# A tuned attention-and-FFN block: the order in which the output projection's weight operands are made, and where one constant load and one bank wait stand

## The reference

```
xn   = layernorm(x)
q, k, v = split(xn @ w_qkv)                  # 32 query heads, 8 key/value heads, D = 128
s    = (q @ k.T) / sqrt(128) - slope[head] * sqrt(i - j), masked where j > i
attn = softmax(s) @ v
out  = x + attn @ w_o                        # attn: 2048 x 4096, w_o: 4096 x 1024
         + xn @ W.T + b + lora(xn, top-1 rank by a gate)
```

## Time and profile before

| | us |
|---|---|
| median of 3 runs (2544.09 to 2546.38) | 2545.13 |
| the profiled execution's own time | 2546.86 |
| its span, first to last instruction | 2545.1 |
| projections, up to the last step's end | about 1208 |
| attention with the output projection, from there on | about 1337 |
| PE busy / DVE / ACT / POOL | 2422.9 / 1514.5 / 1386.5 / 782.1 |
| mean granted TensorE clock | 0.980 of 2.4 GHz |

### The profile page before, as it was taken

The page is one execution under the profiler, slowest core; times in us unless marked ns, Lnnn a source line. Parts: engine busy times, 40 slices in busy tenths (PEclk is TensorE's granted clock), DMA queues, the critical chain, the costliest instruction groups (busy, mean ns, idle before and its releaser), DMA issues.

```text
span 2545.1 us, 35024 instructions
## 1 busy us (share of the span) xinstructions
PE 2422.9 (95%) x12128; PEld 2057.6 (81%) x12128; DVE 1514.5 (60%) x2817; ACT 1386.5 (54%) x3075; POOL 782.1 (31%) x1030
## 2 busy tenths in 40 slices
PE   5999999997899999999699999999999999999999
PEld 4787888886778888888588788887887878878787
DVE  5657455565656446554566666666666666666665
ACT  4432143334533133333767777677776777777764
POOL 3211000001221000000434545345444454454634
PEclk9999999998999999999899999999999999999999
DMA  4546354555245435454655555554655555655543
GB/s 147 186 133 221 118 181 153 186 207 199 93 143 206 166 134 198 166 198 153 223 186 203 187 194 185 202 194 169 220 187 198 187 175 207 207 182 200 182 166 125
DMA packets 118257, 455.95 MB, mean 179 GB/s; under 512 B 11946, under 2 KB 12090, under 8 KB 109121
## 3 DMA queue, kind: packets, MB, share of 16 engines
q1 hardware_dynamic: 86032, 334.11, 38.0%
q0 software_dynamic: 32048, 119.60, 13.5%
HBM read 276.96 MB, written 176.69 MB: 178 GB/s over the span
## 4 chain that ended last, share of the span: by engine, by line
PE 84%; DVE 5%; ACT 4%; POOL 3%; issue 2%; DMA 2%; ACTq 0%; DVEq 0%; SPq 0%; POOLq 0%
PE ps L636 27%; PE ps L637 26%; PE ps L638 26%; PE ps L823 5%; POOL wo_raw L618 1%; POOL op_lo L594 1%; DMA lora_lo<-lora_s 1%; ACT probs L1023 1%; ACT res_hi L883 1%; ACT pt_hi L883 1%; DVE stats L1132 1%; ACT rows L912 1%; DVE pt_lo L1118 1%; DVE w_lo L1118 1%; DVE res_b L1118 0%
## 5 line engine op out<-in xcount | busy, mean ns | idle before, releaser
L883 ACT ACTIVATE w_hi<-raw 128x1024 fp32r<-128x1024 f32 x196 | 207.3, 1061 | 559.6 <-PE ps L638 440.6
L1118 DVE TENSOR_TENSOR w_lo<-raw,w_hi 128x1024 fp32r<-128x1024 f32 x196 | 239.2, 1224 | 358.6 <-ACT w_hi L883 358.5
L1386 DVE TENSOR_TENSOR acc<-ps,acc 128x512 f32<-128x512 f32 x448 | 298.8, 688 | 256.5 <-issue 229.2
L636 PE MATMUL ps<-x_hi,w_hi 128*128 128x512 f32 x1120 | 436.5, 390 | 0.0
L637 PE MATMUL ps<-x_lo,w_hi 128*128 128x512 f32 x1120 | 435.9, 389 | 0.0
L638 PE MATMUL ps<-x_hi,w_lo 128*128 128x512 f32 x1120 | 435.9, 389 | 0.0
L636 PE MATMUL ps<-wo,op_hi 128*128 128x512 f32 x896 | 366.1, 409 | 45.4 <-DVE wo L1118 45.4
L1023 ACT ACTIVATE probs<-probs,neg_max 128x512 f32<-128x512 f32 (+3 forms) x512 | 284.8, 569 | 175.8 <-DVE neg_max L1355 175.8
L638 PE MATMUL ps<-wo,op_lo 128*128 128x512 f32 x896 | 355.8, 397 | 0.0
L637 PE MATMUL ps<-wo,op_hi 128*128 128x512 f32 x896 | 354.8, 396 | 0.0
L594 POOL TENSOR_TENSOR op_lo<-op_raw,op_hi 128x256 fp32r<-128x256 f32 x256 | 201.9, 800 | 305.9 <-ACT op_hi L883 305.9
(11 more groups left out here) (156 smaller groups left out, 4729.5 us busy)
## 6 DMA issues: line engine op xcount, KB each, us to landing
raw<-w_all SPq DMA_DIRECT2D x70, 1024.0 KB, 5.2
q<-qk_s SPq DMA_DIRECT2D x128, 512.0 KB, 4.0
acc<-acc_s SPq DMA_DIRECT2D x128, 512.0 KB, 5.1
acc_s<-acc SPq DMA_DIRECT2D x112, 512.0 KB, 7.8
qk_s<-res_hi POOLq DMA_DIRECT2D x40, 1024.0 KB, 4.6
qk_s<-res_a POOLq DMA_DIRECT2D x20, 1024.0 KB, 9.0
qk_s<-res_b POOLq DMA_DIRECT2D x20, 1024.0 KB, 5.3
k<-qk_s SPq DMA_DIRECT2D x32, 512.0 KB, 3.6
```

Source lines behind the costliest of these rows:

```text
L636: pe.matmul(to, st_hi, mv_hi, start=start, stop=False, skip_group_check=True)
L883: nc.scalar.activation(to, source, ACT.Copy).then_inc(signal, 1)
L1118: nc.vector.tensor_tensor(to, source, high.bitcast(F32), ALU.subtract).then_inc(signal, 1)
L1386: nc.vector.tensor_tensor(to, fill[f % 2][:, :], to, ALU.add).then_inc(s_acc, 1)
```

## The change

Four edits:

1. Weight operands 5 and 6 change places in `WO_ORDER`, in ACT's tables and in DVE's: 6, a raw block, now has its high ahead of the first exponential in turn 16g+6, and 5, the last sum that POOL makes, has its high at the end of that turn. Their lows change places too.
2. Low 0 goes from `LOWS_MIDDLE` of turn 16g+5 to `LOWS_EARLY` of the same turn: from behind the sum-ups to right behind the transposed ones' lows, ahead of the reciprocals.
3. The load of `dist` goes from POOL's queue to SP's, right behind the loads of unit 0, with the same wait (step 4 of the last matrix done) and a semaphore of its own.
4. TensorE's wait for the banks of the last two steps goes from ahead of `scores(1)` to behind it, ahead of the transposes of unit 0. Of the eight waits, five are left (the other three are made ahead of `scores(0)` anyway).

```
-WO_ORDER = (0, 1, 3, 2, 4, 5, 6)
-HIGHS_FIRST = {10: (4, 5)}
-HIGHS_LAST = {8: (0, 1), 9: (3, 2), 10: (6,)}
-LOWS_EARLY = {10: (2,)}
-LOWS_MIDDLE = {9: (0, 1), 10: (4,)}
-LOWS_LAST = {9: (3,), 10: (5, 6)}
+WO_ORDER = (0, 1, 3, 2, 4, 6, 5)
+HIGHS_FIRST = {10: (4, 6)}
+HIGHS_LAST = {8: (0, 1), 9: (3, 2), 10: (5,)}
+LOWS_EARLY = {9: (0,), 10: (2,)}
+LOWS_MIDDLE = {9: (1,), 10: (4,)}
+LOWS_LAST = {9: (3,), 10: (6, 5)}
...
+                if n == 0:
+                    sp.wait_ge(s_bank, 4 * (number(PAIRS - 1, LAST, 4) + 1))
+                    sp.dma_start(dist[:, :], consts[:, 0:SEQ]).then_inc(s_dist, 16)
                 out_weights(n)
                 sums_in_and_out(n)
...
-                    if m == LAST and pr == PAIRS - 1:
-                        pool.wait_ge(s_bank, 4 * (number(pr, m, 4) + 1))
-                        pool.dma_start(dist[:, :], consts[:, 0:SEQ]).then_inc(s_const, 16)
...
-            for n in (TOTAL - 2, TOTAL - 1):
-                for s in range(4):
-                    pe.wait_ge(*drained(n, s))
             for n in range(UNITS + G + 2):
                 if 1 <= n < UNITS:
                     scores(n)
                 todo = fills(n)
                 for f in todo[:1]:
                     fill_in(*f)
+                if n == 1:
+
+                    pe.wait_ge(*drained(TOTAL - 2, 3))
+                    for s in range(4):
+                        pe.wait_ge(*drained(TOTAL - 1, s))
                 if 1 <= n <= UNITS:
                     transposes(n - 1)
...
-                    dve.wait_ge(s_const, 48)
+                    dve.wait_ge(s_dist, 16)
```

More of the change, by code:

```diff
@@ L158, in block_program @@
         s_const = sem("s_const")
+        s_dist = sem("s_dist")
         s_rows = [sem(f"s_rows{i}") for i in range(TT)]
```

## The result

The changed kernel took 2510.86 us (median of 4 runs, 2510.83 to 2515.75), the kernel before 2545.76 us beside it (4 runs, 2544.09 to 2546.57): ratio 0.9867, 95% interval 0.9854 to 0.9881. Run again later, beside other kernels, it took 2515.03 us (4 runs, 2510.16 to 2515.94), ratio 0.9875, interval 0.9860 to 0.9890. So the change gives 31 to 35 us; the forecast was 25.4, with a range that holds the result. The way was right; one term of the sum, the clock behind the stalls, had the wrong sign, and that makes 7.7 us.

The account below looks back on a forecast made before the run. TensorE's waits for DVE's `wo` lows, chained to POOL's sum 5, and the change-over's wait for `dist` were taken as the bound; 19.6 + 2.0 - 3.2 + 7.0 = 25.4 us off 2545.1 gives 2519.7, say 2520 us, range 2504 to 2530 (forecast proper 2512 to 2527).

Parts of the forecast that it names:

- the clock behind the stalls: TensorE's slow work after the shortened stalls in groups 1 to 7: 0.45 us given back per group, 3.2 us lost.
- The chain of the stall: Before part 2, `pt_hi` comes 2.8 us earlier without POOL's sum 5 ahead; stall 5.96 to 3.1 us, 19.6 us gained.
- What comes last now is low 5 ... cost nothing: Before part 5, low 5 is done in time with 1.1 us to spare, so making it last costs nothing.
- rival (b): The stalls before part 2 shrink by less because low 2 waits for POOL's sum 5: 2527 to 2535 us, chance 0.13.
- Edit 2 at 0: Low 0 earlier in turn 16g+5 was put at 0, between a loss of 0.2 and a gain of 0.3 us per group.
- Group 0: The first group's shorter stall of 3.65 us, bound by late transposes: 2.2 us gain worked out, 2.0 taken.
- The change-over: From projections to attention, an earlier `dist` brings unit 0's transposes forward: 7.8 us worked out, bounds 5 and 8, 7.0 taken.
- the lower clock ... if it falls in that gap: In TensorE's new gap of about 2 us before unit 0's transposes, a slow clock may take up to 2.5 us.
- Nothing behind it is needed sooner: In SP's queue, unit 1's `q` is read a step and a half later, and no later load is needed sooner.
- Rival (a): The clock doesn't fall behind the shorter stalls, or only some: 2500.5 us if none, 2510.5 if half; chance 0.18.
- Rival (c): TensorE reaches part 5 before low 5 is done, a second stall per group; slower than before, up to 2562 us, chance 0.03.
- (d): No change in time: some other load or engine holds the loop and gives all back later; chance 0.04.

Follow-up runs that it names:

- swap: Kernel before with only operands 5 and 6 exchanged in the order and in ACT's and DVE's tables: 2516.14 us against 2545.17, ratio 0.9885.
- longer: Changed kernel with ACT's high 6 done twice, one after the other: 2529.13 us against 2545.58 for the kernel before, ratio 0.9934.
- first4: Changed kernel with high 6 moved to the end of ACT's turn 16g+6: 2503.78 us against 2545.58 for the kernel before, ratio 0.9836.
- change34: Kernel before with only the `dist` load on SP's queue and the bank wait behind `scores(1)`: 2540.30 us against 2545.17, ratio 0.9980.
- low0: Kernel before with only low 0 moved to `LOWS_EARLY` of turn 16g+5: 2545.74 us against 2545.17, ratio 0.9998.
- no_low0: Changed kernel with low 0 put back in its old place: 2512.82 us, ratio 0.9875 to the kernel before.
- dist3: Kernel before with only the `dist` load moved to SP's queue: 2540.39 us against 2545.58, ratio 0.9978.
- wait4: Kernel before with only TensorE's wait for the last banks moved behind `scores(1)`: 2545.23 us against 2545.85, ratio 0.9997.
- after_again: The changed kernel itself, run once more beside the later kernels: 2515.03 us, ratio 0.9875 to the kernel before.
- early2: first4 with POOL's sum 5 earlier in turn 16g+5 and low 2 ahead of the transposed ones' lows: 2490.76 us against 2545.85, ratio 0.9784.

## Why the prediction was right, and where it was not

**The chain of the stall** was right link by link: ACT's wait for POOL's sum gone, `pt_hi` 2.8 us earlier, 5.96 to 3.11 us. swap shows that edit 1 does it, longer and first4 that the stall moves with what stands ahead of the exponential, until DVE's maxima bound it. "What comes last now is low 5 ... cost nothing" was right: all eight waits for `wo` are still one per group, before part 2. Sum 5, called the next in line, ended 1.3 us before low 2 began, so rival (b) failed. change34, without the swap, gave 4.9 us, and swap alone 29: together they make up the whole, within what these runs can tell.

**Edit 2 at 0** was right in time (0.9998). The 0.28 us on the stall that low0 shows is there and is not gained.

**Group 0**: 2.2 us worked out, 2.0 taken; 5.0 were gained between unit 3 and unit 9. The stall went from 3.65 to 2.33 us, not to the 1.4 to 1.6 forecast, and no_low0 and swap, without edit 2, have 3.81 us there: so in group 0 it took edit 2 as well, which the working had not seen. (The 3.65 us before come behind slow work of TensorE at 1252.4 to 1257.8; in low0, change34, dist3 and wait4, which all keep the old order of operands 5 and 6, group 0's stall is 4.84 to 5.63 us.) The larger part is the clock: 5.4 us of slow work behind the stall are gone, which is 2.7 us that the sum didn't have. About 1 us more lies ahead of the stall, where the slow work behind the wait of 2.49 us was at least 5.4 us before and is 3.4 now.

**The change-over**: 7.8 us worked out, 8.2 measured at the transposes of unit 0; 7.0 were taken for the clock's sake, and 4.9 were left at unit 3. What was given back was named as "the lower clock ... if it falls in that gap". It didn't fall there but at unit 3, 15 us on, behind the wait of 1.74 us for `q` (the granted clock was 0.50 from 1224.4 to 1227.6). "Nothing behind it is needed sooner" was true of SP's queue and overlooked the DMA engines: with the drain 8 us earlier, stores and loads that had been apart came together (before, the `q` of unit 3 went out at 1220.29, 10 us behind the weight blocks). In no_low0 and first4 the clock fell in the first gap and no wait for `q` shows; either way unit 3 is 27.4 to 27.9 us behind the end of the projections (29.5 in after_again, where wait and low stretch are longer). Alone the two edits gave 4.9 us (change34), the same as at unit 3 here.

Group 0 and the change-over together came to 9.9 us against 9.0 forecast. That is luck: one term was 2.1 us too high and the other 3.0 too low.

**The clock behind the stalls** is the step that failed, a term of -3.2 us that measured +4.5. "A shorter stall eats less of it" took the slow stretch as given and let TensorE only move in it. low0 shows exactly that for a small move. But the stretch itself can be the short kind: behind the 3.11 us stalls the slow work was 3 us, not the 5.3 to 5.8 that I took from the rows at 2.49 and 3.65 us. A price read behind those two didn't carry over. 1.5 us of lost time a group in place of 2.2 is 0.7 x 7 = 4.9 us; by the periods it is 0.65 x 7 = 4.5 us. With 3.2 us forecast the other way the term was off by 7.7 us, and 25.4 falls short of the measured 31 to 35 by 5 to 10.

**Rival (a)**, the clock that doesn't fall: behind the stalls of 3.11 us it fell in each of the seven groups, so it was wrong as put, and right only for group 0. The measured 2510.86 lies in the stretch given to it (2499 to 2512, with 2510.5 named for half of the groups), just outside the 2512 to 2527 of the forecast, and the later 2515.03 inside that. This is no sign for (a): behind the seven stalls the clock fell every time, for a shorter while. The Trainium skill, page "TensorE: Matmul & The Clock Gate", section "HAM oscillation — how this bites in real kernels", has it that short gaps leave the clock up, and by its figure those of 3.11 and of 2.38 us are short enough. The traces disagree, and the measurement decides: it fell behind 3.11 us seven times of seven and behind 2.38 us five times of seven; behind 0.99 us it never did. **Rival (c)**, a wait for low 5, and **(d)** are refuted by the list of waits and the ratio.

What stays open: what decides between the short and the long slow stretch (longer has both behind equal stalls), and whether it falls at all behind 2.38 us. That the stretch was short is measured; why it was, no run here shows.

## What to carry to other kernels

Where TensorE waits in every period for one operand, follow the chain of releases back to the instruction on the in-order engine that waits for a slower one, and put work there that is ready; then ask the same of the next link, which here (early2: low 2 ahead of `pt_lo`, sum 5 earlier) gave 13 us over first4, more than a third of what the change gave. What is left on ACT's queue in that place counts too: first4, one high fewer there, gave 7 to 11. A stall's price is its length plus the slow clock behind it, and that second part moved in steps here: 0.28 us less were worth nothing, and 2.85 us less were worth 3.5. Whatever is made earlier, list the transfers that it sets off and what they now meet; and before a wait is taken out with a load, ask what else it held back.

## What the runs showed of the hardware that I had not expected

The period of a group took values that the stall alone doesn't give: 163.9 us for stalls of 5.96 and of 5.68 us, 160.4 to 160.7 us for 3.11, alternating 161.7 and 162.7 for 4.21, 158.4 or 159.9 for 2.38, 157.7 for 0.99. TensorE's slow work behind a stall lasted, in the same order, 4.1 to 4.8 us, 4.8 to 5.3, 2.9 to 3.4, 3.2 to 3.4 or 5.4 to 5.7, 0 or 3.4, and 0. And DVE's lows and POOL's tensor-tensor operations slow each other: two `op_lo` took 3.41 us beside lows in the earlier trace rows, where the two ahead of them took 1.45, and the lows took 3.31 us for two, where 2.35 is the time of the pair at 1438.58. Who loses depends on how they lie: in the changed kernel, with the lows apart, a low took 1.21 to 1.34 us, and the POOL operation beside it still 1.55 to 1.73 in place of 0.73.
